# Deformable sampling beside attention: the first corner's products on VectorE instead of ScalarE

## The reference

```python
# layer 0: attention over the 4096 pixels of one image
q = Wq @ xf + bq;  k = Wk @ xf + bk;  v = k
attn = softmax(q^T k / sqrt(128));  out = xf^T + attn @ v

# layer 3: deformable 3x3 convolution
# offsets and a mask come from a convolution; for each of 9 taps and each pixel:
val = corner(y0, x0) * (1-ly)*(1-lx) + corner(y0, x0+1) * (1-ly)*lx \
    + corner(y0+1, x0) * ly*(1-lx)   + corner(y0+1, x0+1) * ly*lx
mod = val * mask
out = relu(bn(einsum('bckhw,ock->bohw', mod, weight) + bias))
```

## Time and profile before

| | |
|---|---|
| median of 3 runs | 5489.43 us (5488.87 to 5501.62) |
| the profiled execution's own time | 5494.56 us |
| its span, first to last instruction | 5492.8 us |
| busy, share of the span | PE 77%, DVE 53%, ACT 32%, POOL 25% |
| mean granted TensorE clock | 0.875 of full |
| moved by DMA | 390.60 MB, 302.06 of them by POOL's gathers |

### The profile page before, as it was taken

One profiled execution on the slowest core, in us unless ns is written; L12 is line 12 of the kernel. 1 busy time (PEld: TensorE's weight loads), 2 busy tenths in 40 slices (PEclk: granted clock), 3 DMA queues, 4 the chain that ended last, 5 costly groups with the idle time before them and its releaser, 6 DMA issues.

```text
span 5492.8 us, 67954 instructions
## 1 busy us (share of the span) xinstructions
PE 4236.3 (77%) x20595; PEld 2615.0 (48%) x20888; DVE 2917.3 (53%) x6732; ACT 1734.9 (32%) x3725; POOL 1394.0 (25%) x1493
## 2 busy tenths in 40 slices
PE   6999789788788759877788777977888786895334
PEld 3777434255555524335555543434555553342233
DVE  4333377455545468555445538835455445772455
ACT  2333412233333322223333333223333334122223
POOL 1000110123333330023323313003333332102664
PEclk9999889799989889879899888988999898996666
DMA  1000000423333300033323320033333330004665
GB/s 35 4 4 4 20 0 0 128 72 108 97 94 95 105 6 1 36 105 98 106 78 105 99 77 0 0 91 90 94 95 97 106 109 23 1 12 133 178 185 151
DMA packets 189334, 390.60 MB, mean 71 GB/s; under 512 B 22550, under 2 KB 104854, under 8 KB 187634
## 3 DMA queue, kind: packets, MB, share of 16 engines
q0 software_dynamic: 92160, 302.06, 19.0%
q1 hardware_dynamic: 97010, 86.53, 5.3%
HBM read 328.97 MB, written 59.53 MB: 71 GB/s over the span
## 4 chain that ended last, share of the span: by engine, by line
PE 56%; another core or an unknown queue 13%; DVE 12%; issue 7%; DVEq 5%; ACT 4%; POOL 1%; POOLq 0%; SPq 0%; DMA 0%; ACTq 0%
PE bank L447 11%; PE bank L563 9%; DVE val L1046 4%; DVE mxc L1024 3%; PE bank L470 3%; PE bank L437 3%; PE bank L436 3%; PE bank L418 3%; PE bank L438 3%; PE bank L439 3%; PE bank L548 2%; DVEq L1048 2%; PE bank L589 2%; PE bank L626 2%
## 5 line engine op out<-in xcount | busy, mean ns | idle before, releaser
L1024 DVE TENSOR_REDUCE mxc<-bank 128x1 f32<-128x512 f32 x1024 | 695.7, 688 | 1148.8 <-remote 651.7
L447 PEld LDWEIGHTS bank<-vt,pt 128*128 128x128 f32 x8192 | 1169.8, 206 | 191.1 <-issue 57.9
L447 PE MATMUL bank<-vt,pt 128*128 128x129 f32 x8192 | 1179.3, 289 | 43.0 <-issue 41.5
L729 ACT ACTIVATE pt<-bank 128x512 f32<-128x512 f32 x1024 | 595.2, 596 | 1365.2 <-PE bank L447 970.6
L1404 POOL DMA_INDIRECT G<-patch_table,idxt x864 | 831.5, 962 | 306.3 <-issue 233.9
L1046 DVE SCALAR_TENSOR_TENSOR val<-G,wt,val 128x128 f32<-128x128 f32 x2592 | 747.5, 346 | 297.4 <-ACT val L740 266.6
L1181 DVE SCALAR_TENSOR_TENSOR G<-xn,vec,G 128x512 f32<-128x512 f32 x736 | 521.8, 748 | 48.4 <-issue 42.0
L418 PE MATMUL bank<-regk,qb 128*128 128x512 bf16 x845 | 354.6, 423 | 168.3 <-DVE mxc L1024 153.3
L436 PE MATMUL bank<-qh,regk 128*128 (+1 forms) x971 | 387.5, 399 | 70.8 <-DVE mxc L1024 32.4
L438 PE MATMUL bank<-qh,regk 128*128 (+1 forms) x1021 | 405.2, 397 | 1.3
L437 PE MATMUL bank<-ql,regk 128*128 (+1 forms) x1000 | 397.7, 398 | 3.9 <-ACT m L723 1.0
(11 more groups left out here) (208 smaller groups left out, 5453.9 us busy)
## 6 DMA issues: line engine op xcount, KB each, us to landing
patch_table<-valt SPq DMA_DIRECT2D x64, 512.0 KB, 7.0
G<-patch_table,idxt POOLq DMA_INDIRECT x864
x_cur<-in_x SPq DMA_DIRECT2D x4, 2048.0 KB, 7.5
attn_out<-ob SPq DMA_DIRECT2D x32, 256.0 KB
x_store<-x_cur SPq DMA_DIRECT2D x4, 2048.0 KB, 6.3
xr<-x_store SPq DMA_DIRECT2D x32, 256.0 KB
out<-fo SPq DMA_DIRECT2D x32, 256.0 KB
regq<-attn_out SPq DMA_DIRECT2D x4, 1792.0 KB, 12.5
```

Of the source, the lines that this page charges most:

```text
L447: last = mm(O[t // 2][:, (t % 2) * (C + 1):(t % 2 + 1) * (C + 1)], pt[:, st % PT_RING, t * 128:(t + 1) * 128], vt[:, st, :], start=(st == ...
L729: A(pt[:, st % PT_RING, :], ST[st % ST_RING][:], ACT.Exp, scale=SCALE).then_inc(s["exp_done"], 1)
L1024: v.reduce_max(mxc[:, t, mc:mc + 1], banks[st % len(banks)][:], AX.X).then_inc(s["mx_red"], 1)
```

## The change

The products of the first corner go from ACT to DVE, and with them the waits for the gathers and for PE's transposes. `interpolate` now makes 36 products in its 7 steps (5, 5, 5, 5, 5, 5, 6): 9 of a tile by a column of weights (`tensor_scalar`), then 27 multiply-adds as before. ACT keeps the copy of the weights, now behind the exponential of step 7t, and raises `c0_rdy` with it. The tail keeps its own code (`tail_corner`, `tail_interpolate`), and so do PE, POOL and SP.

```diff
--- before.py
+++ after.py
@@ -42,7 +42,6 @@
 SCALE = float(C) ** -0.5
 SPT = 7
 CONV_IN, CONV_STEPS = 2, 5
-CORNER_IN, CORNER_STEPS = 5, 2
 DCN_IN, DCN_OUT = 3, 10
 
 
@@ -728,18 +727,10 @@
                 act.wait_ge(s["pv_done"], 32 * B + st + 1)
                 A(pt[:, st % PT_RING, :], ST[st % ST_RING][:], ACT.Exp, scale=SCALE).then_inc(s["exp_done"], 1)
 
-            def first_corner(Gb, g, t, r):
-
-                if r == 0:
-                    act.wait_ge(s["val_rdy"], TB * Gb + t + 1)
-                    act.wait_ge(gathered(t), gather_count(Gb, t))
-                    act.wait_ge(s["tr_ps"], 3 * (TB * Gb + t) + 1)
-                    A(wt[:, t % 2, :], w4t(g, t), ACT.Copy)
-                    act.drain()
-                for k in range(K1 * r // CORNER_STEPS, K1 * (r + 1) // CORNER_STEPS):
-                    last = A(val[:, t % 2, k, :], patches(t, k)[:, 0:C], ACT.Copy, scale=wt[:, t % 2, k:k + 1])
-                if r == CORNER_STEPS - 1:
-                    last.then_inc(s["c0_rdy"], 1)
+            def tile_weights(Gb, g, t):
+
+                act.wait_ge(s["val_rdy"], TB * Gb + t + 1)
+                A(wt[:, t % 2, :], w4t(g, t), ACT.Copy).then_inc(s["c0_rdy"], 1)
 
             def dcn_evacuate(Gb, t, r):
                 e = 3 * t + r
@@ -776,9 +767,9 @@
                     if dcn:
                         for t, r in leaving(st - ST_RING):
                             dcn_evacuate(Gb, t, r)
-                        t, r = (st - CORNER_IN) // SPT, (st - CORNER_IN) % SPT
-                        if 0 <= t < TB and r < CORNER_STEPS:
-                            first_corner(Gb, i, t, r)
+                        t, r = st // SPT, st % SPT
+                        if t < TB and r == 0:
+                            tile_weights(Gb, i, t)
                 if nxt:
                     shift_copy(B + 1, i + 1)
 
@@ -1036,14 +1027,19 @@
 
                 if r == 0:
                     dve.wait_ge(s["c0_rdy"], TB * Gb + t + 1)
-                for o in range(3 * K1 * r // SPT, 3 * K1 * (r + 1) // SPT):
-                    corner, k = 1 + o // K1, o % K1
-                    if corner > 1 and k == 0:
+                    dve.wait_ge(gathered(t), gather_count(Gb, t))
+                    dve.wait_ge(s["tr_ps"], 3 * (TB * Gb + t) + 1)
+                for o in range(4 * K1 * r // SPT, 4 * K1 * (r + 1) // SPT):
+                    corner, k = o // K1, o % K1
+                    if corner and k == 0:
                         dve.drain()
                     src = patches(t, k)[:, corner * C:(corner + 1) * C]
                     wgt = wt[:, t % 2, corner * K1 + k:corner * K1 + k + 1]
                     dst = val[:, t % 2, k, :]
-                    v.scalar_tensor_tensor(dst, src, wgt, dst, ALU.mult, ALU.add)
+                    if corner == 0:
+                        v.tensor_scalar(dst, src, wgt, None, ALU.mult)
+                    else:
+                        v.scalar_tensor_tensor(dst, src, wgt, dst, ALU.mult, ALU.add)
                 if r == SPT - 1:
                     dve.drain()
                     dve.sem_inc(s["val_rdy"], 1)
```

## The result

| | before | after |
|---|---|---|
| median | 5495.52 us (4 runs, 5488.87 to 5505.89) | 5593.59 us (4 runs, 5578.05 to 5603.84) |
| ratio | | 1.0174, 95% interval 1.0141 to 1.0207 |
| the profiled execution | 5494.56 us | 5600.32 us |
| mean granted TensorE clock | 0.875 | 0.863 |

What follows compares the result with a forecast made beforehand. Each tile's cycle was taken as the gather's 13.9 us plus DVE's work behind the stall. Five more multiply-adds there (92.6 us) and tile 0 (13.2) summed to +105.8 us, so 5595 us; the range was 5550 to 5715.

Steps and rivals of the forecast that it cites:

- The cycle: Attention blocks with sampling: a tile takes the gather's 13.9 us, then DVE's remaining work, 7.1 us before the change.
- The term of the five multiply-adds: Four steps behind the stall: 21 multiply-adds instead of 16, 1.47 us later for tiles 1, 2 and 3, 92.6 us.
- DVE's first products at nothing: First two steps of a tile: nine products, 1.9 us, lie under DVE's idleness; for tile 0 under slower PE; cost nothing.
- Tile 0: Its end, outside a stall: last steps 0.11 us too long plus two multiply-adds, 0.52; 0.63 x 21 = 13.2 us.
- The last block at zero: Last block of each of three samples, without reductions: taken as zero, 20 us either way.
- as many as before: Last block of a sample: tile 0 is ready earlier, gathers and stalls lie elsewhere but their number stays.
- The sum: All terms together: +105.8 us, giving 5595 us against the median of 5489.43.
- POOL's rival: DVE's new products hold up POOL's nine gather DMAs: 1.25 us x 63 = 79 us more, 5674 us; chance 0.17.
- PE's clock: PE's 1.7 us waits for tiles 1 and 2 lower its clock: some 84 us more, 5680 us; chance 0.10.
- No change: The stall is a fixed loss following the engines; DVE's own chain counts, +0.15 us a tile, 5499 us; chance 0.12.
- Faster: PE gets one step further before the stall, leaving 6.43 us behind it instead of 7.03: -25 us, 5464; chance 0.08.

Runs made afterwards that it cites:

- ScalarE's corner and 21 late: Kernel before, its 27 multiply-adds a tile shared out 2, 2, 2, 5, 5, 5, 6, so 21 stand behind the stall: 5604.67 us, ratio 1.0195.
- VectorE's corner and 16 late: Changed kernel, its 36 operations a tile shared out 7, 7, 6, 4, 4, 4, 4, so 16 stand behind the stall: 5492.63 us, ratio 0.9983.
- 4 late: Kernel before, ScalarE keeping the first corner, multiply-adds shared out 7, 8, 8, 1, 1, 1, 1, so 4 stand behind the stall: 5419.30 us, 0.9848.

## Why the prediction was right, point by point

**The cycle: right, by a mechanism that two runs isolate.** "13.9 us and then what DVE still has to do" gave 22.5 us for the changed kernel. It is 22.41 in the mean, 22.4 to 22.6 in 56 of 63 intervals. DVE's last wait of over 0.25 us ends 13.83 us behind the copy in the mean over the 63, and 13.85 in the kernel before. Moving five operations across the stall makes and unmakes the loss whatever engine has the corner. Why PE's signals are late during a gather was left open in the prediction and is open still.

**The term of the five multiply-adds: right.** 92.6 us were predicted, 91.2 came in the profiled pair. The 8.50 us behind the stall is the figure of the prediction to the hundredth.

**DVE's first products at nothing: right.** They take 0.284 us and follow one another every (1.06 - 0.284) / 4 = 0.194 us, 0.289 and 0.205 by the estimate. For tiles 1 to 3 they lie ahead of the stall; for tile 0 they lie in steps 3 and 4, where the reductions stand 3.69 us apart before and after.

**Tile 0: its own part right, with a larger one beside it that I can't explain.** At its last steps the medians over the 18 intervals give 0.11 and 0.47 us, 0.58 and not 0.63. But the interval from tile 3 to tile 0 grew by 1.46, and the other part, 0.87 us in the mean (3.33 and 4.20), lies between the first two reductions behind tile 3's stall, ahead of any product. In the run with ScalarE's corner and 21 late, that same place is 0.4 us *shorter* than in the kernel before (2.95), and in it the interval grew by 0.23 only. So it doesn't go with the number behind the stall. The place varies from 0.61 to 4.62 us within the kernel before alone, so some of this may be scatter; what it goes with stays open.

**The last block at zero: wrong, -29 us.** The step that failed is "as many as before". The gathers are as many, but in each of these blocks PE's idle time falls from 15.4, 13.3 and 15.2 us to 6.1, 6.1 and 7.9. The last block has no reductions, and DVE is free as soon as tile 3 of the block before is done. Before, it then waited for ACT, whose products come behind the exponentials of steps 5 and 6; the timeline of DVE in sample 1's last block, of the kernel before:

```profile
1854.37 7.50 DVE L1046 SCALAR_TENSOR_TENSOR val<-G,wt,val 128x128 f32<-128x128 f32 x27 [19.41 <-ACT val L740]
```

and after the change:

```profile
1875.48 1.85 DVE L1040 TENSOR_SCALAR val<-G,wt 128x128 f32<-128x128 f32 x9 [6.23 <-issue]
1877.41 7.50 DVE L1042 SCALAR_TENSOR_TENSOR val<-G,wt,val 128x128 f32<-128x128 f32 x27
```

Here the wait for ACT was on the path: from tile 3's copy to tile 0's it is 31.2 us before and 20.0 after (29.2 and 20.0 in the other two samples). The runs separate this gain as well: with VectorE's corner and 16 late, the last blocks take 76.9 to 77.4 us; with ScalarE's corner and 21 late 82.7 to 83.3, and with 4 late 84.6 to 85.8. That is -20 us for VectorE's corner with 16 late, enough for the 0.9983, which is -9 us.

**The sum, right in part by cancelling.** Predicted for the three attentions were 105.8 us; they grew by 92, of it 91 from the five multiply-adds and +26 and -29 from the two places above, which nearly cancel. The tail's 10 us more, in untouched code, brought the profiled pair to 105.8 all the same, and that is luck. So is a part of 5595 against 5593.59: the medians differ by 98 us and not by 105.8, and the median before lay 6 us above the one that I had added to.

**POOL's rival: refuted.** The rows of L1400 show a mean of 957 ns (962 before), and 234.7 / 768 = 0.31 us between two, with the TENSOR_SCALARs now beside them. By their place in the burst, the first DMA took 0.996 us (1.006 before) and the second 0.949 (0.946), so no hold-up hides in the mean; the stall's end has not moved. The Trainium skill (SBUF — State Buffer, "Who interferes with whom") would have DVE's `tensor_scalar` on two ports keep GpSimd out for an instruction, its descriptor writing too; that cost doesn't show in this trace. The profile doesn't name the mode in which these float32 instructions ran, so the rule itself isn't tested.

**PE's clock: refuted for a wait of this length.** Behind the 1.91 us wait at 1482.33 the matmul of 512 columns takes 0.38 us, the transposes 0.55, as at the full level; behind tiles 1 and 2 the matmul is slower than that in 2 of 42 cases. Tile 3, which the prediction left out of this rival, is another matter: PE's wait there grew from 2.2 to 3.3 us (medians), and the three transposes behind it took over 0.7 us, as at a lower clock, in 20 of 21 blocks after the change and in 8 before. It lies ahead of a stall whose end did not move.

**No change** (5499 us) is refuted by the result, and its reason by the run with ScalarE's corner and 21 late: DVE's work is the same there as before, and the time grows by 103 us. The stall is no fixed loss that follows the engines' work. **Faster** did not come: in the profiled execution of the changed kernel no step more got through ahead of the stall, two reductions stand between the copy and the stall in 62 of 63 intervals. On the second chip some do, and there the change costs no less.

## What to carry to other kernels

Where a stall ends at a time that one engine's work doesn't move, work ahead of it is free as far as it fits, and work behind it is paid in full until another engine sets the pace: count an engine's operations on either side before asking how many there are. A removed wait is worth what follows it on the path; here 131 us of waiting for ScalarE were worth nothing in 21 blocks, and 45 us of it in each of the three last blocks were worth some 10. And an even spread over steps was the wrong choice beside this stall: moving operations ahead of it made the kernel 0.5 to 1.7% faster than before, by a table of eight numbers.

## What the runs showed of the hardware that I had not expected

- PE's signals reach DVE and ACT late while POOL sends indirect gathers, until 13.9 us behind the copy of the indices for nine (8.2 at most for five), and with a quarter of the bytes (POOL's queue at 132.19 MB and not 302.06) just as late. Nine DMAs end some 12.0 us behind the copy. Why the signals wait isn't settled by any run here.
- Two chips differ in it: on the second, single steps get through during a gather, the kernel before takes 5358 to 5370 us and not 5502, and the value of moving work ahead of the stall is about half or less, 0.5 to 0.8% and not 1.5 to 1.7%.
